# Fetching every message of the second graph convolution by one-hot products

## The reference, cut to what matters

```python
h = x @ W1                                   # 6250 x 8
msg = h[src] * norm[:, None]
out = segment_sum(msg, dst) + b              # first convolution, 8 features
h = relu(layernorm(out))                     # still 8 features
# second convolution: the same gather and sum of 8-feature rows, then W2 (8 x 512)
out = relu(segment_sum((h @ W2)[src] * norm[:, None], dst) + b2)
x = x + out * size_factors
x = x + ffn(layernorm(x))                    # 512 -> 1408 -> 512
```

## Time and profile before

| | us |
|---|---|
| median of the runs | 3361.59 |
| span of the profiled execution | 5135.2 |
| stage A | 0 to 191 |
| stage B | 191 to 1099.7 |
| stage C, opening up to the first FFN product | 1099.7 to 2161 |
| stage C, FFN | 2161 to 3388 |
| stage D, sums | 3388 to 4800 |
| stage D, experts | 4800 to 5135.2 |

### The profile page before, as it was taken

How to read it: one execution, slowest core, us unless ns; L and a number is a source line. 1 busy time by engine, 2 the same in 40 slices (tenths; PEclk the granted TensorE clock), 3 DMA queues, 4 the chain that set the end, 5 groups by cost and what they waited for, 6 DMA issues and landing times. The chain is left out here.

```text
span 5135.2 us, 61590 instructions
## 1 busy us (share of the span) xinstructions
PE 2982.4 (58%) x17153; PEld 2061.9 (40%) x17154; DVE 1973.4 (38%) x3813; ACT 1285.4 (25%) x2086; POOL 2000.5 (39%) x2038
## 2 busy tenths in 40 slices
PE   7511179631111000299989999956667666665789
PEld 7400068620000000177777777732232232322477
DVE  9300079750000000166666566632223223232366
ACT  3200057410000000144444444420011111111344
POOL 0377700037777777300000000035555455554244
PEclk9555589755555555599999999977888788887799
DMA  3101023210000000022333233345555556555465
GB/s 101 39 5 11 4 64 96 61 41 3 3 3 3 3 3 3 6 91 88 107 95 102 88 104 100 100 151 168 168 170 161 163 173 182 170 161 158 134 193 155
DMA packets 241523, 466.48 MB, mean 91 GB/s; under 512 B 77093, under 2 KB 107069, under 8 KB 241235
## 3 DMA queue, kind: packets, MB, share of 16 engines
q0 software_dynamic: 107264, 235.06, 17.4%
q1 hardware_dynamic: 133970, 227.93, 14.2%
HBM read 395.90 MB, written 73.45 MB: 91 GB/s over the span
## 5 line engine op out<-in xcount | busy, mean ns | idle before, releaser
L1971 POOL DMA_INDIRECT rows<-xn_rows,srcT x784 | 744.2, 949 | 665.4 <-DVEq L2441 440.7
L129 POOL DMA_INDIRECT msg_c<-hid_rows,srcT x744 | 770.0, 1035 | 245.0 <-issue 236.5
L2122 PE MATMUL pV<-rows,oh 128*128 x2240 | 645.5, 435 | 331.6 <-issue 262.2
L2122 PEld LDWEIGHTS pV<-rows,oh 128*128 x2240 | 238.7, 107 | 724.1 <-issue 576.2
L1197 PE MATMUL pG<-parts,los 128*128 128x200 bf16 x2640 | 308.6, 258 | 322.7 <-issue 322.7
L1487 PE MATMUL gates<-xT,wgu_hi 128*128 128x384 f32 (+1 forms) x1848 | 472.3, 377 | 39.2 <-ACT gate_sum L1585 20.6
L1954 POOL IOTA bases<- 128x49 f32 x1 | 0.2, 188 | 1269.8 <-POOLq L387 1269.8
L1518 PE MATMUL accs<-wd,hT 128*128 128x512 f32 x1617 | 405.4, 398 | 16.2 <-DVE hT L1733 16.2
L129 POOL DMA_INDIRECT msg_b<-hid_rows,srcT x344 | 345.5, 1004 | 110.2 <-issue 105.6
L1197 PEld LDWEIGHTS pG<-parts,los 128*128 128x128 bf16 x2640 | 240.9, 100 | 356.0 <-issue 354.2
L1487 PEld LDWEIGHTS gates<-xT,wgu_hi 128*128 128x128 f32 x1848 | 336.4, 190 | 105.4 <-issue 60.9
(11 more groups left out here) (432 smaller groups left out, 5300.1 us busy)
## 6 DMA issues: line engine op xcount, KB each, us to landing
wd<-wd_rows SPq DMA_DIRECT2D x154, 512.0 KB
we<-in_L_ffn_expert_w SPq DMA_DIRECT2D x16, 1024.0 KB
lo<-lo_rows SPq DMA_DIRECT2D x110, 128.0 KB
x_rows<-xr SPq DMA_DIRECT2D x49, 256.0 KB, 4.0
xn_rows<-pair SPq DMA_DIRECT2D x49, 256.0 KB
rows<-xn_rows,srcT POOLq DMA_INDIRECT x784
res<-x_rows SPq DMA_DIRECT2D x49, 256.0 KB
x_rows<-agg SPq DMA_DIRECT2D x49, 256.0 KB
```

The source lines that it names most:

```text
L129: nc.gpsimd.indirect_dma_start(msg[:, c, :], None, table, bass.IndirectOffsetOnAxis(ap=srcT[:, c:c + 1], axis=0)).then_inc(landed[u % 2], 16)
L1971: nc.gpsimd.indirect_dma_start(rows[:, u % RING, c, :], None, xn2_rows, bass.IndirectOffsetOnAxis(ap=srcT[:, u * Q + c:u * Q + c + 1], axi ...
L2122: last = nc.tensor.matmul(pV[:, ds(to, 1), :].rearrange("p a d -> p (a d)"), oh[:, ds(to, 1), c, :].rearrange("p a d -> p (a d)"), rows[:, ...
```

## The change

MC goes from 10 to C // 4 = 196, so that all 784 chunks of the second convolution are fetched by product. The gathers of stage C on GpSimd go, with their two semaphores, and so does the table in HBM that they read (`hid2_rows`), with its store at the end of stage B. The gathers of stages B and D stay.

```diff
-MC = 10
-assert 4 * MC % V == 0 and MC <= M
+MC = C // 4
+assert 4 * MC == C
...
-        hid2_rows = dram("hid2_rows", (NT * P, H), F32)
...
                 sp.wait_ge(s["hid2"], 1)
-                sp.dma_start(hid2_rows.rearrange("(p t) f -> p t f", t=NT), hid[:]).then_inc(s["stored"], 16)
-                sp.wait_ge(s["stored"], 16)
...
-        landed = [sem(f"c_landed{h}") for h in range(2)]
...
-                gather_units(nc, pool, hid2_rows, srcT, msg, landed, s["msg"], 4 * MC // V)
                 pool.sem_inc(s["msg"], U // VS)
```

## The result

The changed kernel takes 3797.51 us, the median of two runs (3790.98 and 3804.03), against 3361.59 us before: a ratio of 1.1294, with a 95% interval of 1.1264 to 1.1324. The change costs 13%, or 436 us (425 to 445 by the interval). The forecast was 3800.

What follows compares the result with a forecast made beforehand. The prediction took the recorded stall in stage C's opening as mostly absent from runs, the gathers as hidden beside the FFN, and TensorE as the new opening's bound: 3361.6 + 515 - 75 gives about 3800 us, range 3640 to 3880.

Steps and rivals of the forecast that it cites:

- Step 1: Opening of stage C before: the traced 1061 us are mostly a recording stall; a run holds at most 414 us.
- The floor of 2947 us: Least run time before outside stage C's opening, summed from A, part of B, FFN, D's sums and experts.
- The rival on the other side: Stage C's opening: the stall is real in runs, opening falls by 546 us, time to 2816 us; chance 0.03.
- Step 2: Stage C's opening before, as run: 75 us, with 50 us of it for 40 gathers.
- Step 3: Gathers beside the FFN: 1.25 us each, under the threshold of 1.56 us, so removing them gives 0.
- Rival 1: Stage C: gathers held the FFN back before, so the rise is only 101 to 440 us; named 3650 us; chance 0.08.
- Step 4: Check of the rest of the run before: stage B 454 us, D's sums left with 1080 us.
- Step 5: Stage C's opening with the change: 515 us, with 196 groups at 2.40 us, 470 us, bound by TensorE.
- B's pace of 2.72 us: Dearer price of a product group, from stage B's rows: +63 us, 3865 us, kept inside the range.
- Step 6: Reordered loads, number loads and the dropped table store: 0, at most 3 us less.
- The sum: Stage C's opening after less before, 515 - 75 = +440 us on the run.
- the span of the changed kernel's profile: Profiled execution: opening falls from 1061 to 515 us, so span falls from 5135 to about 4590 us.

Runs made afterwards that it cites:

- the second of before: The kernel before, unchanged, profiled once more: 3352.14 us, span 3350.4 us.
- both fetches: The changed kernel with the table stored again and the 744 gathers issued into a scratch buffer nobody reads: 3804.72 us, ratio to before 1.131.
- no gathers: The kernel before without stage C's 744 gathers, messages of chunks 40 to 783 filled with zeros: 3344.94 us, ratio 0.9937.
- the kernel with slowed gathers: The kernel before with every second gather of stage C issued twice, the copy into scratch: 3647.06 us, ratio 1.0835.
- the kernel with three products: The changed kernel with three products for a chunk in stage C instead of seven: 3726.88 us, ratio to before 1.1072.
- M = 120: The kernel before with 120 groups fetched by product in stage B instead of 110: 3338.02 us, ratio 0.992.

## Why the prediction was right, point by point

**Step 1, the stall is no part of a run: right.** The floor of 2947 us, built from stages full of their own work, allowed the opening at most 414 us where the trace had 1061; it had 69. It was no strict floor: as run, A took 180 us and the experts 310, 36 us less than it held, and the FFN 27 us more; its 345 us to spare covered that. The rival on the other side, 2816 us, rested on those 1061. That one decision set the sign of the forecast.

**Step 2, the opening before, 75 us: 69.** The sum held 50 us for gathers of tile 3, with the unit's announcement after the next issue. Nothing in the opening waited for gathers (68 us without them, the late start of that run taken off). It lasts as long as ten groups of products and what follows them: 10 x 2.40 = 24, with the same 46 us of start and end that after shows (516.3 - 470). The wait was argued from the code alone and put tile 3's build at 53 us into the stage (1153 less 1099.7); it came at 48.5 (738.1 less 689.6), behind ten groups and three builds. So the term was wrong, and that the sum was only six microseconds off is luck: two paths of nearly the same length ran side by side.

**Step 3, the gathers beside the FFN cost nothing: nearly.** They took 1.33 us each, not the 1.25 taken from the rows, and still stayed under the threshold. But the step looked at the mean pace, and the cost sits at the start: two waits of 15.5 us in all before tiles 5 and 6, and an FFN that is 10 us shorter without them. The prediction saw one of them, put it at some 8 us and left it in the range instead of in the sum; it measured 13.8 us. Rival 1, which named 3650 us, is refuted by three recordings (the second of before, both fetches, no gathers); the mechanism itself is real, and the kernel with slowed gathers shows it at 1.94 us a chunk. As to the page "SBUF — State Buffer" of the Trainium skill, by whose figure the prediction estimated 2306 us for 744 caught gathers: the stage C of before does not show that, with a median of 945 ns and a longest gather of 2239 ns.

**Step 4, the rest of the budget: two errors that cancelled.** Stage B was put at 454 us as run and D's sums at 1080; they are 510 and 1027. For B the 344 gathers were taken at 1.25 us and 18 us added; they need (668.8 - 181.1)/343 = 1.42 us on the mean, and are slowest beside the tile sums (below). D was only what was left over, so B's error went into it with the other sign. Neither number entered the forecast, since only the difference of the openings did. As a check of the whole it looked better than it was.

**Step 5, the opening after, 515 us: 516.3.** 2.40 us a group held for all 196, at clock 1.00, with TensorE the bound, as the kernel with three products shows; from the end of the last pick (1180.9 + 1.0) to the first FFN product are 36 us, where 35 were taken. B's pace of 2.72 us was rightly left as a bound.

**Step 6, small edits: 0.** The opening is explained without them.

**The sum** gave +440, the runs +436 and the traces +447 in the opening and -10 in the FFN. That it came within 4 us is in part luck: the opening before was taken 6 us too long, and the 10 us of the FFN were taken as 0.

**Wrong: the span of the changed kernel's profile.** The forecast was 4590 us, it is 3802.3. The step took the stall for something that recording does to every kernel that gathers, so that B and D would stall in the next profile too. It did not recur in the other eleven recordings. The cause it named has a number wrong as well. Packets, MB and share of the queue that carries the gathers, in the stalled recording of before and in that of the kernel without stage C's gathers:

```profile
q0 software_dynamic: 107264, 235.06, 17.4%
```

```profile
q0 software_dynamic: 83456, 232.27, 24.8%
```

The difference of 23808 packets is 32 for each of the 744 gathers, where the prediction spoke of 128 transfers, and the two unstalled recordings of before hold 107264 too: the execution that stalled had no more of them. The floor argument did not need a cause, and the text should have stopped at "this recording". Why that execution stalled, and whether records were its cause, stays open; the sentence of the page "NOTIFIC — the notification-queue block" (section 7.1) neither gained nor lost by it, as no run here shows that block.

## What to carry to other kernels

When a profile's span and the timed runs differ by half, first find stages that are full of their own work, add them up as a floor, and see how much of a hole the runs can hold at all; then profile the same kernel again, since the second recording here settled what the first had left to argument. Work that a long stage covers is nearly free as long as its pace stays under the stage's own (here gathers at 1.33 us, against an estimated 1.57); ask besides whether the stage's first steps want it sooner than that pace brings it (here 15.5 us of waits); replacing it by work on the engine that bounds the next stage costs its full length (196 groups of 2.40 us). Balance two ways of fetching where both end late, in stage B (120 groups, 0.8%), and not where one of them is hidden.

## What the runs showed of the hardware

An indirect DMA of 128 rows keeps GpSimd 0.94 us, and the next starts 0.30 us later. Beside the tile sums of stage B it takes 1.67 us. Timeline of the second recording of before, two such gathers:

```profile
596.61 1.49 DVE L213 TENSOR_TENSOR onehot_b<-numbers_b,rels 128x2560 bf16<-128x2560 bf16 x1
597.25 1.67 POOL L129 DMA_INDIRECT msg_b<-hid_rows,srcT  x1 [0.30 <-issue]
...
598.58 1.49 DVE L213 TENSOR_TENSOR onehot<-numbers_b,rels 128x2560 bf16<-128x2560 bf16 x1
599.22 1.67 POOL L129 DMA_INDIRECT msg_b<-hid_rows,srcT  x1 [0.30 <-issue]
```

Thirteen microseconds after that, with no build beside it, the same instruction of the same recording:

```profile
610.36 0.94 POOL L129 DMA_INDIRECT msg_b<-hid_rows,srcT  x1 [0.30 <-issue]
611.60 0.94 POOL L129 DMA_INDIRECT msg_b<-hid_rows,srcT  x1 [0.30 <-issue]
```

The gathers start 1.97 us apart beside the one-hot builds, and in step with them (596.61 and 598.58), against 1.24 beside none. The gather begun at 597.25 lies 0.85 us beside one build (to 598.10) and 0.34 us beside the next (from 598.58). It holds over the whole stage: of 51 gathers that have a build beside their first 0.94 us, 49 take more than 1.1 us (mean 1.68), and of the other 293 only 28 do (mean 1.00). The builds set the rhythm and not the gathers: with M = 120 the last gather starts at 617.2, and the sums of tiles keep ending 1.98 us apart after it (619.95, 621.93, 623.90). That the build is what holds a gather still rests on these coincidences; no run took the builds away. It would explain in part why the last gathers of B end so late, and why 10 more product groups there pay.
